# Edge sums of a graph kernel with the selection as stationary operand, copied and turned back

## The reference

```
W = einsum('rb,bio->rio', coeff[l], basis[l])          # 8 relations
h = segment_sum(all_h[etype, src] * norm, dst) + bias[l] # relu after the first
x = layernorm(x + h)
agg = segment_sum(h[src], dst) / deg                   # three times
h = relu(agg @ W_agg[l] + h @ W_self[l] + b_hid[l])
x = layernorm(x + h @ W_out + b_out)
```

## Time and profile before

| | |
|---|---|
| median of 3 runs | 1962.34 us |
| the profiled execution | 1962.86 us, span 1961.0 us |
| PE matmul busy | 1707.9 us (87%), 10003 records |
| DVE busy | 1229.3 us (63%) |
| ACT busy | 495.2 us (25%), 1040 instructions |
| POOL busy | 1275.7 us (65%), 1307 instructions |
| chain that ended last, by engine | PE 58%, DMA 24%, POOL 9%, issue 4%, DVE 4% |
| granted clock of PE, mean | 0.969 |

### The profile page before, as it was taken

How to read it: one execution, slowest core, us unless ns; L and a number is a source line. 1 busy time by engine, 2 the same in 40 slices (tenths; PEclk the granted TensorE clock), 3 DMA queues, 4 the chain that set the end, 5 groups by cost and what they waited for, 6 DMA issues and landing times.

```text
span 1961.0 us, 32300 instructions
## 1 busy us (share of the span) xinstructions
PE 1707.9 (87%) x10003; PEld 1424.5 (73%) x10003; DVE 1229.3 (63%) x4083; ACT 495.2 (25%) x1040; POOL 1275.7 (65%) x1307
## 2 busy tenths in 40 slices
PE   5687788988889988888889989999988889999997
PEld 4666676777777776676777777777777777777775
DVE  8978767786777777576777755454554554322344
ACT  2012121211121112122232225444112212533332
POOL 7777777777777777777777777777777775000011
PEclk9989999999999999999999989999998999999999
DMA  8334454444344334444444446554444442210011
GB/s 265 105 111 120 131 151 110 116 109 112 109 114 109 110 110 116 116 133 127 126 138 120 132 129 166 159 147 137 123 117 123 124 131 79 77 50 0 11 41 46
DMA packets 148682, 223.13 MB, mean 114 GB/s; under 512 B 79261, under 2 KB 104508, under 8 KB 148508
## 3 DMA queue, kind: packets, MB, share of 16 engines
q0 software_dynamic: 61152, 166.68, 30.3%
q1 hardware_dynamic: 51260, 40.65, 7.0%
q10 hardware_dynamic: 36096, 13.70, 2.6%
HBM read 203.66 MB, written 17.27 MB: 113 GB/s over the span
## 4 chain that ended last, share of the span: by engine, by line
PE 58%; DMA 24%; POOL 9%; issue 4%; DVE 4%; DVEq 0%; ACT 0%; ACTq 0%; POOLq 0%
PE bank L1163 21%; DMA RY<-H,si 12%; DMA RY<-in_x,si 12%; PE bank L1005 10%; PE bank L1426 9%; POOL RY L390 9%; PE bank L725 3%; PE bank L1055 2%; PE bank L988 2%; PE bank L1392 2%; PE bank L1436 2%; PE bank L1498 1%; PE bank L987 1%; DVE RY L669 1%; PE bank L1070 1%
## 5 line engine op out<-in xcount | busy, mean ns | idle before, releaser
L1163 PE MATMUL bank<-RY 128*128 128x128 f32 x5088 | 737.8, 288 | 191.2 <-DMA RY<-in_x,si 106.0
L1163 PEld LDWEIGHTS bank<-RY 128*128 128x128 f32 x5088 | 665.4, 198 | 272.6 <-DMA RY<-in_x,si 127.7
L390 POOL DMA_INDIRECT RY<-in_x,si x627 | 639.0, 1019 | 194.5 <-issue 142.6
L390 POOL DMA_INDIRECT RY<-H,si x630 | 599.3, 951 | 191.9 <-issue 142.0
L669 DVE TENSOR_SCALAR RY<-iot,c,wgt 128x128 f32<-128x128 f32 x1290 | 451.6, 360 | 320.7 <-PE bank L1163 319.2
L834 ACT CAST RY<-bank 128x320 uint8<-128x320 f32 x215 | 91.1, 424 | 559.1 <-PE bank L988 539.5
L1426 PE MATMUL bank<-Ar,hs 125*128 125x500 f32 x800 | 203.9, 405 | 0.0
L661 DVE TENSOR_TENSOR RY<-RY,bank 128x256 f32 x430 | 179.4, 417 | 38.5 <-issue 26.0
L547 DVE TENSOR_SCALAR RY<-iotN,bcol 128x320 bf16<-128x320 f16 x645 | 201.9, 313 | 0.0
L1487 POOL TENSOR_TENSOR x1b<-x1b,bo 125x256 f32<-125x256 f32 x20 | 14.7, 735 | 273.2 <-DMA x1b<-X 273.2
L1005 PE MATMUL bank<-RX,RY 128*128 128x256 f32 x704 | 182.5, 387 | 7.5 <-issue 3.7
(11 more groups left out here) (159 smaller groups left out, 1536.7 us busy)
## 6 DMA issues: line engine op xcount, KB each, us to landing
RY<-H,si POOLq DMA_INDIRECT x630, 2.8
RY<-in_x,si POOLq DMA_INDIRECT x627, 2.8
Ad<-RY ACTq DMA_DIRECT2D x215, 40.0 KB
A<-Ad SPq DMA_DIRECT2D x22, 312.5 KB, 3.4
D<-Ad SPq DMA_DIRECT2D x14, 305.2 KB
RX<-in_basis ACTq DMA_DIRECT2D x2, 2048.0 KB, 20.0
AhG<-Ad SPq DMA_DIRECT2D x6, 610.4 KB
H<-RY SPq DMA_DIRECT2D x23, 128.0 KB
```

The costliest lines, as they stand in the source:

```text
L390: e.indirect_dma_start(G[0:k, slot, :], None, table, bass.IndirectOffsetOnAxis(ap=index[0:k, t:t + 1], axis=0)).then_inc(s_land[slot], 16)
L1163: mm = e.matmul(bank[2 + wg % 3][:, c * 128:(c + 1) * 128], rows, S[0:k, n % NSS, :], start=(i == 0 and not ahead), stop=(i == TA - 1))
```

## The change

The sums take S as stationary operand and all 256 features of the rows as moving one: three matmuls a window with (relation, destination) down the partitions, each of which counts up s_sum. ACT copies the 256 columns out of PSUM (`act_sums`, at the step t with t % 3 = 0 behind the window's last tile) into one of four buffers Y, which lie over di and ei, index tables that are used no more by then. PE turns the two halves with transposes into the other half of the same bank (`pe_turn`, at t % 3 = 1, ahead of the sums and products of that step); DVE's addition, at its old step, waits for them and reads that half. In the plan the groups 1 to 19 of layer 0 have all their steps two later; in layer 1 the groups 0 to 15 have k = 10, 11, 12 and 13 later by 1, 4, 5 and 8, and the units of the first eight groups of blocks start eight steps later (those of the eighth every 5 steps and not every 6); those from step 572 on stay. The branches for rows fetched by SP and ACT, whose lists are empty, are gone.

```diff
+LATE = {10: 1, 11: 4, 12: 5, 13: 8}
+            late = LATE if l == 1 and g < 16 else {}
+            if l == 0 and 0 < g < NW - 2:
+                first += 2
-                tile = end + 2 + (k + 1) // 2 if l == 0 and g == NW - 2 else first + by * k
+                tile = end + 2 + (k + 1) // 2 if l == 0 and g == NW - 2 else first + by * k + late.get(k, 0)
-        first, by = (92 + 60 * gi, 6) if gi < 8 else (572, 3) if gi == 8 else (602, 2)
+        first, by = (100 + 60 * gi, 6 if gi < 7 else 5) if gi < 8 else (572, 3) if gi == 8 else (602, 2)
+        Y = [v[:, 256 * i:256 * i + 256].bitcast(F32) for v in (di, ei) for i in range(2)]
@@ dve_add
-            e.wait_ge(s_sum, l * T + min(T, TA * w + TA))
-            e.tensor_tensor(o, o, bank[2 + wg % 3][:, 0:256].rearrange("p (q c) -> p q c", c=16), ALU.add).then_inc(s_za, 1)
+            e.wait_ge(s_turn, wg + 1)
+            e.tensor_tensor(o, o, bank[2 + wg % 3][:, D:2 * D].rearrange("p (q c) -> p q c", c=16), ALU.add).then_inc(s_za, 1)
@@ act_layer
+                if t >= TA and t % TA == 0 and t <= T:
+                    act_sums(e, l, t // TA - 1)
                 for g, k in STEPS[l].get(t, []):
@@ pe_sums_of, and new functions
-            for c in range(2):
-                ...
-                    mm = e.matmul(bank[2 + wg % 3][:, c * 128:(c + 1) * 128], rows,
-                                  S[0:k, n % NSS, :], start=(i == 0 and not ahead), stop=(i == TA - 1))
-                    if c == 1:
-                        mm.then_inc(s_sum, 1)
+            for i in range(TA):
+                ...
+                e.matmul(bank[2 + wg % 3][:, 0:D], S[0:k, n % NSS, :], rows, start=(i == 0 and not ahead),
+                         stop=(i == TA - 1)).then_inc(s_sum, 1)
+        def act_sums(e, l, w):
+            wg = l * NA + w
+            e.wait_ge(s_sum, l * T + min(T, TA * w + TA))
+            if wg > 3:
+                e.wait_ge(s_turn, wg - 3)
+            e.copy(Y[wg % 4], bank[2 + wg % 3][:, 0:D]).then_inc(s_whole, 1)
+        def pe_turn(e, l, w):
+            wg = l * NA + w
+            e.wait_ge(s_whole, wg + 1)
             for c in range(2):
+                mm = e.transpose(bank[2 + wg % 3][:, D + c * 128:D + (c + 1) * 128], Y[wg % 4][:, c * 128:(c + 1) * 128], idn[:, :])
+            mm.then_inc(s_turn, 1)
@@ pe_layer
                     pe_sums_of(e, l, t)
+                if t >= 4 and t % TA == 1 and t - 2 < T:
+                    pe_turn(e, l, (t - 4) // TA)
```

More of the change, by code:

```diff
@@ L359, in program @@
                                     "y", "bn", "sq", "gather", "xd", "md"))
-        s_hcopy = k_cp
+        s_hcopy, s_whole, s_turn = k_cp, k_row, k_st
         s_xin, s_xhi, s_xlo, s_hat, s_hsrc, s_hone, s_hsum, s_hrow = [k_own, k_y, k_bn, k_sq], k_ix, k_rows, [k_prod, k_mm], k_z, k_x, k_tr, k_ht
@@ new lines, in pe_sums_of @@
+            if ahead:
+                e.matmul(bank[2 + wg % 3][:, 0:D], Cs[:, w % 2, :], h1w[:, (NW - 1) % 2, :], start=True, stop=False)
+            for i in range(TA):
+                n, k = l * T + t - TA + 1 + i, edge_rows(t - TA + 1 + i)
+                if n in PLACE:
+                    rows = G[0:k, PLACE[n] % NG, :]
+                    e.wait_ge(s_land[PLACE[n] % NG], 16 * (PLACE[n] // NG + 1))
+                else:
+                    q = HOT_TILES.index(n)
+                    rows = GH[0:k, q % 2, :]
+                    e.wait_ge(s_hrow, q + 1)
+                e.matmul(bank[2 + wg % 3][:, 0:D], S[0:k, n % NSS, :], rows, start=(i == 0 and not ahead),
+                         stop=(i == TA - 1)).then_inc(s_sum, 1)
```

## The result

Changed 1981.58 us (1980.9 to 1984.72, 4 runs), before 1961.94 beside it: ratio 1.0104, interval 1.0093 to 1.0116. 19.6 us slower, four times the 4.8 that were forecast, outside the range.

The account below looks back on a forecast made before the run. POOL was taken to bound both layers. Boundary 1.4 plus tail 1.6 and 1.8 made 4.8 us on the median of 1962.34, so 1967.1 us; the forecast's own range was 1964 to 1971, the range with rivals 1962.0 to 1977.0.

Parts of the forecast that it names:

- the chain's 21% on the sums: PE's line L1163 in the chain of waits: 21%, called misleading, as POOL has long been ordered to fetch those rows.
- rival (c): POOL runs dry: PE exposed 0.40 us a window, gathers 5.5 us late in layer 1's middle, 1975.4 us; chance 0.18.
- 69 x 0.17 = 11.7 us, under 7.8 + 5.2 = 13.0: Middle of layer 1, 1190 to 1450: 69 windows' net PE cost fits into PE's old waits; cost 0.
- With other PE work between in most windows: Transposes: PE work between copy and transposes in most windows, so a window costs PE 0.17 us net, not 0.4.
- the same instructions fall under POOL's gathers: Moved steps of layer 0 and moved units: same instructions, under POOL's gathers; cost 0.
- Start: Steps 3 to 18: reserve before a gather shrinks from 2.4 to 0.7 us, no gather late; cost 0.
- Boundary: Between the layers: copy behind a cast delays the second last group's product, lengthening POOL's pause; 1.4 us, lowest 0.3.
- Tail: From 1595.52: turning of windows costs 1.6 us, window 213's copy behind the square root 1.8 us.
- rival (a): Tail: PE's clock stays up as transposes shorten its long landing wait, giving back 2.2 us, 1964.9 us; chance 0.16.
- (b): The new waits cost nothing, only the tail's turning does, 1.6 us: 1963.9 us; chance 0.07.
- (d): Gathers collide less with DVE's 18 long comparisons, 0.5 us less each, 9 us faster: 1958.1 us; chance 0.05.

Follow-up runs that it names:

- wide_only: Changed kernel without ACT's copy and the transposes, sums added unturned, wide sums and new plan kept: 1966.84 us against 1964.23 before, ratio 1.0009.
- plan_only: Kernel before with its old sums and only the new plan of steps and units: 1963.68 us against 1962.52 before, ratio 1.0011.
- units_101: Changed kernel with every unit before step 572 ordered one step later: 1970.06 us, ratio 1.0053 to the kernel before.
- old_steps: Changed kernel with layer 1's later posts put back where they were, moved units kept: 1971.41 us, ratio 1.0057 to the kernel before.
- after_again: The changed kernel itself, measured again: 1985.86 us against 1960.7 for the kernel before, ratio 1.0124.
- early_oldplan: Changed kernel with the old plan and ACT's copy ordered at the sums' step: 1966.79 us against 1960.7 before, ratio 1.0036.
- sums_only: Changed kernel's new sums with the old plan of steps and units: 1974.61 us against 1964.23 before, ratio 1.0046.
- turn_plus3: Changed kernel with transposes and addition three steps later, except each group's last window: 1972.43 us, ratio 1.0047 to the kernel before.
- copy_early: Changed kernel with ACT's copy at the top of the step of its window's sums: 1970.95 us, ratio 1.0045 to the kernel before.
- early_plus3: Changed kernel with ACT's copy at the sums' step and transposes three steps later: 1974.14 us against 1964.23 before, ratio 1.0047.
- plus3_double: Changed kernel with transposes three steps later and each pair issued twice: 1977.67 us against 1964.23 before, ratio 1.0064.
- wait_only: Changed kernel without the transposes, ACT's copy and PE's wait kept, sums added unturned: 1966.53 us against 1962.52 before, ratio 1.0018.

## Why the prediction was wrong, and where it was right

The bound was read rightly: POOL sets the layers, its work was unchanged, the wide sums alone showed nothing late (wide_only, 2.6 us above the kernel before), and the chain's 21% on the sums meant no gain. The sign followed, and rival (c), POOL runs dry in the middle of layer 1, is what happened. I gave it 0.18, and sized it at 5.5 us for 12.5.

*The step that failed: "69 x 0.17 = 11.7 us, under 7.8 + 5.2 = 13.0. PE stays in time, barely ... Cost 0".* The mis-sized term is what a window costs PE. The transposes were 0.22 us a pair, as stated:

```profile
1657.13 0.38 PE L1172 MATMUL bank<-idn,ei 128*128 128x128 f32 x2
...
1657.35 1.03 PE L1012 MATMUL bank<-RY 128*128 128x256 f32 x4
```

But PE's waits for copies in that stretch were 24.7 us over 66 windows, 0.37 each, so 0.54 a window and not 0.17, nor the 0.40 of rival (c). The old waits that could be used up, landings 7.8 and L640 5.2, are gone altogether.

How that becomes 12.5 us is seen over the same 69 windows in both traces, from the first matmul of window 94's sums in layer 1 to that of window 163's: length, busy time of each engine, clock, DMA share, GB/s.

```profile
1198.38:1456.14 257.76, 237.45 (x1447) 199.00 (x1446) 134.48 (x385) 97.34 (x199) 195.30 (x206) 0.97 0.49 141
1210.30:1480.60 270.30, 242.57 (x1172) 187.35 (x1171) 138.29 (x386) 118.29 (x267) 195.50 (x207) 1.00 0.47 133
```

PE needs 12.5 us more: 5.1 more busy, and 27.7 idle for 20.3. The old waits are landings 8.1, L640 5.2, one addition 1.1, and a term that the prediction left out, 5.5 for the casts of the degrees:

```profile
PE bank L1122 <- ACT RY L880: 5.5, 8, 0.9
```

Of the new ones copies are 25.9 and these casts 1.3. Two things made the change cheaper than 0.54 a window: 4.2 us of cast waits were used up as well, and the granted clock was 1.00 for 0.97, which is worth about 6 us of PE's work here (an estimate: 237.5 us busy x 0.026, with a mean of 0.974 before). The reserve takes nothing off these 12.5 us, since it was used up before they begin: the least reserve is 7.5 us between 1000 and 1050 and 0.9 between 1100 and 1150, and the first late gather of the middle starts at 1166.5. So it was right to set PE's cost a window against its slack, but the price of a window was wrong, and rival (c) took 9.1 us of reserve off lateness that, in the change, came after the reserve was gone.

*Why the price was wrong.* "With other PE work between in most windows" was said of a plan that moves that work. In the old plan all 80 units before step 572 stand at steps with t % 3 = 2, between sums and transposes; the new start at 100 puts 74 of them at t % 3 = 1, behind the transposes (counted from `unit_plan`). With 0.9 us a unit, PE's cover for the copy falls from 1.35 to 0.92 us a window, by the plan. LATE puts k = 12 of 16 groups in a step with t % 3 = 2, whose three operations of ACT come right before the copy. My text priced the moved steps at nothing, since "the same instructions fall under POOL's gathers": true of plan_only and false beside the new waits. units_101 shows the first, old_steps the second, each worth 14 to 16 us of time beside after_again. Matching every pair's wait in this stretch with what ACT had just done, row by row, 11.2 us stood behind degree casts, 6.3 behind the clearing of ZA, 3.9 behind k = 11 and 12; in units_101 the first is 4.4.

The reserves make the account plain: 8.6 in the kernel before, 9.5 early_oldplan, 9.2 wide_only, 9.0 plan_only, 8.4 sums_only, 8.1 turn_plus3, 6.6 copy_early, 6.5 early_plus3, 5.7 plus3_double, 4.0 old_steps, 3.3 wait_only, 1.3 units_101, and nothing left in the change. So a form with 1.3 us left shows nothing in the gathers, and the change, which takes both halves of the moved plan, shows 12.5 us.

*Start: reserve 0.7 forecast, cost 0.* Measured late by 0.8 (0.6 to 2.0 in the other forms with copies and transposes, 0 in wait_only). The identities did start behind the first copy,

```profile
23.11 0.37 ACT L1165 COPY di<-bank 128x256 f32<-128x256 f32 x1 [1.59 <-PE bank L1156]
...
23.38 2.97 ACT L806 ACTIVATE RY<-idn,cf 128x128 f32<-128x128 f32 x9
```

1.8 us later than in the earlier trace rows and not 1.0, since the copy waits for all of the first sums, whose six passes took 2.93 us by PE's timeline, for 1.29 later in the run; why they are so slow there is not shown.

*Boundary: 1.4 forecast, pause 2.0 longer.* The product came at 819.89 after a wait of 0.70 behind transposes that had waited 1.25 for the copy, as the earlier trace rows made expect:

```profile
818.76 0.44 PE L1172 MATMUL bank<-idn,di 128*128 128x128 f32 x2 [1.25 <-ACT di L1165]
...
819.89 1.13 PE L1012 MATMUL bank<-RX,RY 128*128 128x256 f32 x4 [0.70 <-DVE RY L666]
...
833.10 0.33 SPq L1232 DMA_DIRECT2D H<-RY  x1
```

The store left 0.7 us later than before (833.10 for 832.42), the first gather from H1 started 1.13 later (836.78 for 835.65); the other 0.86 of the longer pause is layer 0 having ended that much earlier. So the order cost 1.13 us there for the 1.4 forecast. The pause is not explained over all forms, though: 1.7 to 2.0 us in turn_plus3, copy_early, plus3_double and early_oldplan, 3.5 to 3.7 in wait_only, early_plus3, units_101 and old_steps, 4.99 in sums_only.

*Tail: 3.4 forecast, 4.4 measured.* The copy of window 213 stands behind the square root as worked out, and the wait for it is 1.27 us. The timeline of all engines, against the earlier trace rows:

```profile
1664.46 0.29 ACT L907 ACTIVATE sm<-sm,eps 128x1 f32<-128x1 f32 x1 [1.66 <-DVE sm L634]
1664.67 0.35 ACT L1165 COPY di<-bank 128x256 f32<-128x256 f32 x1
...
1665.07 0.44 PE L1172 MATMUL bank<-idn,di 128*128 128x128 f32 x2 [1.27 <-ACT di L1165]
...
1667.75 0.37 ACT L1165 COPY di<-bank 128x256 f32<-128x256 f32 x1 [2.73 <-PE bank L1156]
...
1668.84 0.42 DVE L666 TENSOR_TENSOR RY<-RY,bank 128x256 f32 x1 [2.50 <-PE bank L1172]
...
1669.32 1.99 PE L1012 MATMUL bank<-RY 128*128 128x256 f32 x8 [0.70 <-DVE RY L666]
```

From the square root to the product of the last group it was 1651.22 - 1648.10 = 3.12 us, now 1669.32 - 1664.46 = 4.86: 1.74 us for the 1.8 that were forecast, and copy_early took 2.0 away. The remaining 1 us over forecast I can't place. The tail also varies with PE's last long wait for a landing; see rival (a).

*Rivals.* (a) did not apply as put: there was still one long wait for a landing, 3.59 us before 1609.00, and around its end the granted clock fell as before. It came true in part in units_101, whose queues in the tail are the same: there the last two long waits are 1.99 and 1.89 us, the clock is down for half as long, and the tail behind the last gather is 316.9 us, 3 us less than in the change. First the change, then units_101:

```profile
1605.00:1610.00 5.00, 1.41 (x4) 0.84 (x4) 0.00 (x0) 0.12 (x1) 3.78 (x5) 0.76 0.81 202
1610.00:1615.00 5.00, 5.00 (x15) 4.02 (x14) 2.11 (x6) 1.25 (x3) 3.78 (x5) 0.55 0.64 190
```

```profile
1590.00:1600.00 10.00, 8.12 (x36) 6.53 (x35) 3.51 (x9) 3.56 (x9) 7.57 (x9) 0.84 0.73 195
```

The clock gave away 3.4 us in the first and 1.6 in the second, which can account for at most 1.8 of the 3 us; old_steps, which lost 1.7 us so (0.66 in 1600 to 1605), still has a tail of 319.1. So the clock alone doesn't set the tail.

(b) and (d) fell: 159 us of waits, and POOL's work stayed the same (637.3 us in layer 0 for 639.0). What (d) suspected is there all the same, in both kernels. Each of DVE's 18 long comparisons holds up a gather that runs beside it, as here in the kernel before:

```profile
391.75 2.83 DVE L711 TENSOR_TENSOR hot<-hT 125x2560 fp32r<-125x2560 f32 x1
391.83 3.57 POOL L390 DMA_INDIRECT RY<-in_x,si  x1 [0.30 <-issue]
```

The 18 gathers beside them last 2.4 to 3.6 us for the usual 0.95. Since POOL is the bound, these some 35 us lie on the path that sets the time, more than the whole change cost, and the change left them as they were (18 gathers of 2.4 us and more in its trace too).

*Open.* All forms with copies and transposes lie 6 to 11 us above the kernel before even where the middle is clean, 13 with doubled transposes; start, boundary and tail of their profiles give 2.4 (early_oldplan) to 7. The gathers' sum differs by 8 us between these profiles (1251.0 to 1259.1, the largest in wide_only, without copies or transposes) and by 3.9 between the two of the changed kernel, and single profiles can't tell how much of that belongs to the form. Whether the harm of LATE is the place of k = 12 alone was not tried.

## What to carry to other kernels

When an edit adds a hand-over inside an ordered queue, price it with the order that the same edit leaves, not with the old one: count, by residue of the step, what stands between the two ends of the new wait. An engine with a few us of reserve in front of the bound hides every single cost, and gives all of it back at the step that uses up the last of it; so add the costs up against the reserve before calling any one of them free. Waits count as much as work in that account: PE was full with 90% busy and 10% waiting.

## What the hardware showed that I had not expected

Two pairs of transposes issued back to back took 0.60 us for 0.38 of one (plus3_double, and its like in the earlier trace rows): 0.11 us each in a row, though one lasts 0.29. And PE's granted clock was 1.00 in the stretch of 69 windows above for 0.97 before (mean of the run 0.987 for 0.969), though PE's busy share fell there from 92% to 90% and it worked a fifth fewer passes (1172 records for 1447). In that stretch, then, neither a higher busy share nor more passes went with the higher clock; what did is not shown.

A comparison of DVE over 125 x 2560 numbers, 2.83 us, stretched a gather of POOL from 0.95 us to between 2.4 and 3.6, 18 times out of 18 in the kernel before.
